# A Flamingo layer on one core: context columns by DMA and 32x32 blocks instead of TensorE, norms on ScalarE, head division in pairs

## The reference

```python
def reference(x, ctx, g_xattn, g_ffn, w_q, b_q, w_k, b_k, w_v, b_v, w_o, b_o, w_f, b_f):
    q, k, v = layernorm(x) @ w_q.T + b_q, ctx @ w_k.T + b_k, ctx @ w_v.T + b_v      # 16 heads of 32
    attn = softmax(where(causal, q @ k.T / sqrt(32), -inf))                         # per batch and head
    x = x + tanh(g_xattn) * ((attn @ v) @ w_o.T + b_o)
    y = fp6_blocks(layernorm(x))                   # scale = max|block of 32| / 7.5, nearest value of 6 bits
    return x + tanh(g_ffn) * (y @ fp6_blocks(w_f).T + b_f)
```

## Time and profile before

| | |
|---|---|
| profiled execution, its own time | 1426.4 us |
| its span, first to last instruction | 1424.4 us |
| TensorE (PE) busy | 1381.7 us, 97% |
| VectorE (DVE) busy | 1102.1 us, 77% |
| ScalarE (ACT) busy | 894.7 us, 63% |
| GpSimd (POOL) busy | 854.3 us, 60% |
| share of the 16 DMA engines, main queue | 41.6% |
| mean granted TensorE clock | 0.989 |

### The profile page before, as it was taken

One profiled execution on the slowest core, in us unless ns is written; L12 is line 12 of the kernel. 1 busy time (PEld: TensorE's weight loads), 2 busy tenths in 40 slices (PEclk: granted clock), 3 DMA queues, 4 the chain that ended last, 5 costly groups with the idle time before them and its releaser, 6 DMA issues.

```text
span 1424.4 us, 35124 instructions
## 1 busy us (share of the span) xinstructions
PE 1381.7 (97%) x10844; PEld 1220.1 (86%) x10844; DVE 1102.1 (77%) x4219; ACT 894.7 (63%) x2969; POOL 854.3 (60%) x1387
## 2 busy tenths in 40 slices
PE   6899999999999999999999999999999999999976
PEld 6788888888888888888888888888888888888865
DVE  5778787887788878778788778788778887877763
ACT  4566666666666666666666666666666666666651
POOL 2455665566665666666656566556666566666662
PEclk9999999999999999999999999999999999999988
DMA  8444434444434444434444443444443444443310
GB/s 255 107 112 106 117 93 120 115 128 107 119 90 118 118 125 118 108 94 116 118 119 124 108 114 97 116 117 128 107 119 93 115 117 125 118 111 90 86 51 29
DMA packets 156103, 159.10 MB, mean 112 GB/s; under 512 B 28176, under 2 KB 130576, under 8 KB 155920
## 3 DMA queue, kind: packets, MB, share of 16 engines
q1 hardware_dynamic: 155920, 156.87, 41.6%
HBM read 39.33 MB, written 16.78 MB: 39 GB/s over the span
## 4 chain that ended last, share of the span: by engine, by line
PE 91%; DVE 3%; SPq 2%; issue 1%; ACT 1%; POOL 1%; DMA 1%; DVEq 0%; ACTq 0%; POOLq 0%
PE proj L483 20%; PE proj L484 20%; PE proj L485 20%; PE pT_ps L533 12%; PE oT_ps L550 6%; PE proj L577 6%; PE s_ps L522 4%; PE s_ps L523 2%; SPq L342 1%; DMA all_probs<-in_L_xattn_w_v 1%; ACT all_probs L660 1%; DVE all_probs L807 0%; DMA q_stack<-q_hi 0%; POOL x L448 0%; POOL x L444 0%
## 5 line engine op out<-in xcount | busy, mean ns | idle before, releaser
L410 POOL TENSOR_TENSOR all_probs<-all_probs,rden 128x128 f32<-128x128 f32 (+1 forms) x1024 | 505.0, 514 | 473.3 <-DVE rden L867 472.1
L660 ACT ACTIVATE all_probs<-all_probs,neg_max 128x128 f32<-128x128 f32 (+1 forms) x1024 | 458.7, 451 | 396.7 <-DVE neg_max L807 396.5
L807 DVE CUSTOM_DVE_ANT_0 all_probs<-s_ps,causal 128x128 f32<-128x128 f32 (+1 forms) x1024 | 321.7, 351 | 164.4 <-PE s_ps L523 160.8
L533 PE MATMUL pT_ps<-ident,all_probs 128*128 128x128 f32 x1536 | 264.5, 282 | 6.6 <-POOL all_probs L410 4.3
L660 ACT ACTIVATION_READ_ACCUMULATOR all_probs<-all_probs,neg_max 128x1 f32 x1024 | 195.5, 191 | 0.0
L919 DVE COPY all_probs<-pT_ps 128x384 f32<-128x384 f32 x256 | 139.0, 543 | 66.5 <-PE pT_ps L533 66.5
L533 PEld LDWEIGHTS pT_ps<-ident,all_probs 128*128 128x128 f32 x1536 | 160.4, 142 | 21.7 <-issue 12.7
L522 PE MATMUL s_ps<-k_stack,q_stack 96*128 96x256 f32 x512 | 154.8, 302 | 2.8 <-DVE neg_max L807 2.2
L483 PE MATMUL proj<-cT_hi,wk_hi 128*128 128x256 f32 x512 | 153.2, 299 | 1.9 <-DVE cT_lo L861 1.1
L483 PE MATMUL proj<-aT_hi,wq_hi 128*128 128x256 f32 x512 | 148.0, 289 | 0.4 <-ACT vs L675 0.4
L484 PE MATMUL proj<-cT_lo,wk_hi 128*128 128x256 f32 x512 | 142.4, 278 | 0.0
(11 more groups left out here) (125 smaller groups left out, 3487.3 us busy)
## 6 DMA issues: line engine op xcount, KB each, us to landing
k_stack<-k_hi SPq DMA_DIRECT2D x512, 64.0 KB, 2.0
q_stack<-q_hi SPq DMA_DIRECT2D x512, 64.0 KB, 2.1
xs<-in_x SPq DMA_DIRECT2D x32, 512.0 KB, 4.2
cs<-in_ctx SPq DMA_DIRECT2D x32, 512.0 KB, 6.1
k_stack<-k_lo SPq DMA_DIRECT2D x256, 64.0 KB, 2.0
q_stack<-q_lo SPq DMA_DIRECT2D x256, 64.0 KB, 2.1
out<-x SPq DMA_DIRECT2D x32, 512.0 KB, 3.0
vs<-in_L_xattn_w_k SPq DMA_DIRECT2D x2, 512.0 KB, 7.0
```

Source lines behind the costliest of these rows:

```text
L410: last = nc.gpsimd.tensor_tensor(p, p, rden[:, sd, t, h:h + 1].to_broadcast([P, (1 + t) * P]), ALU.mult)
L533: last = nc.tensor.transpose(pT_ps[h % 2][:, m * P:(m + 1) * P], probs[:, h % P_RING, m * P:(m + 1) * P], ident[:, :])
L660: last = nc.scalar.activation(probs[:, h % P_RING, cols], probs[:, h % P_RING, cols], ACT.Exp, scale=-1.0, bias=neg_max[:, sd, t, h:h + 1] ...
L807: last = nc.vector.tensor_tensor_reduce(probs[:, h % P_RING, cols], s_ps[h % 2][:, cols], causal[:, (1 - t) * P:], 1.0, MASKED, ALU.add, A ...
```

## The change

- The context is no longer transposed on TensorE. Four DMAs bring it from HBM as `c_quads`: group g of 32 partitions holds columns 128g to 128g+127 of all tokens, in pieces of 512 bytes. VectorE's `transpose` (32x32 blocks, one instruction of 128x512 per half) makes `cols`; ScalarE writes `cT_hi` from it and GpSimd subtracts for `cT_lo` (before: VectorE, from PSUM).
- Both norms go from VectorE to ScalarE (`normalised`, Identity with a scale and a shift per token); GpSimd computes the shift with one more small instruction after each power.
- Reciprocals and divisions take two heads at once, in even slots; probabilities are transposed two heads at once, in even slots, 4 slots after the even head's score; the ring of probabilities has 6 places, not 4.
- q and k are stacked together: 24 DMAs of twice the size per batch instead of 48.
- x is loaded a second time for the residual, and `add_o` is added in place in `x1` (`xb`); `blk_up` is computed directly, with one instruction fewer per half. xT and dT have tiles of their own.
- New order of units over the slots, banks given out in turn, new slots for each stage (`AT`), weights spread over steps 0 to 2, loads of k, q and v weights from ScalarE's queue.

(Comments that name the engine are put in for the reader.)

```diff
-UNITS = [("cT", 0, 1), ("cT", 1, 1), ("q", 1, 2), ("dT", 0, 4), ("k", 0, 1), ("dT", 1, 4), ("f", 0, 4), ("xT", 0, 1),
-         ("f", 1, 4), ("xT", 1, 1), ("o", 0, 3), ("o", 1, 3), ("q", 0, 1), ("v", 0, 1), ("k", 1, 1), ("v", 1, 1)]
-SLOT_PARTS = (2, 4, 4, 1, 1, 5, 4, 2, 3, 4, 4, 1, 3, 3, 3, 2)
+UNITS = [("k", 1, 2), ("dT", 0, 4), ("q", 1, 2), ("f", 0, 4), ("xT", 0, 1), ("o", 0, 3), ("xT", 1, 1), ("k", 0, 1),
+         ("dT", 1, 4), ("q", 0, 1), ("o", 1, 3), ("f", 1, 4), ("v", 0, 1), ("v", 1, 1)]
+SLOT_PARTS = (2, 4, 2, 1, 2, 4, 2, 4, 2, 4, 3, 1, 2, 4, 3, 4)
+AV_SLOTS = (11, 3)
+AT = {      # stage: (steps after its batch's first, slot) of each half
+    "cT": ((1, 1), (1, 3)), "cT_hi": ((1, 3), (1, 5)), "cT_lo": ((1, 3), (1, 5)),
+    "moments": ((0, 11), (0, 13)), "rstd": ((0, 12), (0, 14)), "xn": ((0, 13), (0, 15)),
+    "xb": ((3, 3), (3, 7)), "rstd2": ((3, 8), (3, 14)), "y": ((3, 8), (3, 14)), "amax": ((3, 9), (3, 15)),
+    "scales": ((3, 11), (4, 0)), "scaled": ((3, 12), (4, 1)), "grid": ((3, 13), (4, 2)),
+    "xd": ((3, 15), (4, 4)), "xf": ((3, 9), (3, 15)),
+}
...
+            def stack_pair(b, half):            # SyncE
+                sp.wait_ge(left["k"], 2 * b + half + 1)
+                sp.wait_ge(left["q"], 2 * b + half + 1)
...
+                for j in range(GROUP):
...
+                    for r, (q_at, k_at) in enumerate(((0, 2), (1, 2), (0, 3))):
+                        sp.dma_start(stack[r * DK:(r + 1) * DK, :, at:at + 2, :].bitcast(F32),
+                                     qk[its, q_at:k_at + 1:k_at - q_at].bitcast(F32)).then_inc(stacked[half][j], 16)
...
+            def deviation(n, t, mom, var, rstd, shift, va, rs):        # GpSimd
+                pool.wait_ge(va, n)
+                nc.gpsimd.tensor_tensor(rstd[:, t:t + 1], var[:, t:t + 1], minus_half[:, t:t + 1],
+                                        ALU.pow).then_inc(rs, 1)
+                pool.wait_ge(rs, 2 * n - 1)
+                nc.gpsimd.tensor_scalar(shift[:, t:t + 1], mom[:, t, 0:1], rstd[:, t:t + 1], -1.0, ALU.mult,
+                                        ALU.mult).then_inc(rs, 1)
...
+                for s in range(SLOTS):                                 # GpSimd's step
+                    for b, t in due("rstd2", i, s):
+                        deviation(2 * b + t + 1, t, mom2, var2, rstd2, shift2, va2, rs2)
+                    for b, t in due("rstd", i, s):
+                        deviation(2 * b + t + 1, t, mom1, var1, rstd1, shift1, va1, rs1)
+                    b, h = pair_summed(i, s)
+                    if s % 2 == 0 and live(b):
+                        divide(b, h)
...
+                for s in range(SLOTS):                                 # TensorE's step
+                    if live(i - 2):
+                        scores(i - 2, s)
+                    units(i, s, 0, SLOT_PARTS[s] // 2)
+                    b, h = pair_turned(i, s)
+                    if s % 2 == 0 and live(b):
+                        transpose_probs(b, h)
+                        transpose_probs(b, h + 1)
+                    units(i, s, SLOT_PARTS[s] // 2, SLOT_PARTS[s])
+                    for b, r in weighed(i, s):
+                        weigh_values(b, r)
...
+                for s in range(SLOTS):                                 # ScalarE's step
+                    for unit_ended in ended(i, s):
+                        unit(*unit_ended)
+                    for b, r in put_out(i, s):
+                        output_hi(b, r)
+                    for b, t in due("y", i, s):
+                        second_norm(b, t)
+                    for b, t in due("grid", i, s):
+                        to_grid(b, t)
+                    for b, t in due("cT_hi", i, s):
+                        upper("cT", b, t, cT_hi, (("k", 2 * b), ("v", 2 * b)))
+                    if live(i - 2):
+                        exponentials(i - 2, s)
+                    b, h = pair_turned(i, s)
+                    if s % 2 == 0 and live(b):
+                        act.wait_ge(pT_done, HEADS * b + h + 2)
...
+                        nc.scalar.activation(probsT[:, h % AV_HEADS + 1, :], pT_ps[1][:, 0:3 * P],
+                                             ACT.Copy).then_inc(pT_odd, 1)
...
+                for s in range(SLOTS):                                 # VectorE's step
+                    if live(i - 2):
+                        maxima(i - 2, s)
+                    b, h = pair_summed(i, s)
+                    if s % 2 == 0 and live(b):
+                        reciprocals(b, h)
+                    b, h = pair_turned(i, s)
+                    if s % 2 == 0 and live(b):
+                        dve.wait_ge(pT_done, HEADS * b + h + 1)
...
+                        nc.vector.tensor_copy(probsT[:, h % AV_HEADS, :], pT_ps[0][:, 0:3 * P]).then_inc(pT_even, 1)
+                    for unit_ended in ended(i, s):
+                        unit(*unit_ended)
+                    for b, t in due("amax", i, s):
+                        block_maxima(b, t)
```

More of the change, by code:

```diff
@@ L38 @@
 FP6_BLOCK = 32
+QUAD = 32
 MASKED = 1e37
@@ new lines, in ended, with chunks_at, chunks_before, columns @@
+                if at_slot == (slot - 1) % SLOTS and part == PARTS[kind] - 1 and live(i - lag):
+                    yield kind, half, i - lag, proj[place_of[kind, 2 * (i - lag) + half] % BANKS]
+        def chunks_at(i, s):
+            for chunk in WEIGHT_TURNS.get((i, s), ()):
+                yield TURNED.index(chunk), *chunk
+        def chunks_before(i, s):
+            return chunks_at(i, s - 1) if s else chunks_at(i - 1, SLOTS - 1)
+        def columns(kind, t):
+            return cols[:, COLS.index((kind, t)), :, :]
@@ new lines, in weight_bank, with whole, pair_turned, pair_summed @@
+        def weight_bank(u):
+            return proj[place_of["w", u] % BANKS][:, :].rearrange("p (c k) -> p c k", c=KC)
+        def whole(w, rows=KC):
+            return 1 + max(TURNED.index((w, m)) for m in range(rows))
+        def pair_turned(i, s):
+            return i - (2 if s >= PT_LAG else 3), (s - PT_LAG) % SLOTS
+        def pair_summed(i, s):
+            return i - (2 if s >= 2 else 3), (s - 2) % SLOTS
+        def weighed(i, s):
+            for r, slot in enumerate(AV_SLOTS):
+                if s == slot and live(i - 2 - r):
+                    yield i - 2 - r, r
@@ L305, in fused_kernel, with put_out @@
+        def put_out(i, s):
+            for r, slot in enumerate(OUT_SLOTS):
+                if s == slot and live(i - 2 - r):
+                    yield i - 2 - r, r
         block = es.enter_context(nc.Block())
@@ L475, in _ @@
+            for i in range(STEPS):
+                step(i)
         @block.tensor
@@ L604, in unit, with units, step @@
                     last.then_inc(done[kind], 1)
-            def units(i, s):
-                for (u, part), its_slot in zip(parts, slot_of):
+            def units(i, s, first, end):
+                for u, part in parts[slot_of.index(s) + first:slot_of.index(s) + end]:
                     kind, half, lag = UNITS[u]
-                    if its_slot == s and live(i - lag):
-                        unit(u, part, kind, half, i - lag, i)
-            def step(i, ph):
-                if at(i, 2):
-                    pe.wait_ge(wlo_ok, len(WEIGHTS) * KC)
-                    pe.wait_ge(add_ok, 1)
+                    if live(i - lag):
+                        unit(part, kind, half, i - lag)
+            def step(i):
                 for s in range(SLOTS):
@@ L828, in unit, with first_moments @@
-            def unit(u, kind, half, b, pl, sd):
-                bank = proj[BANKS[u]]
-                if kind in ("q", "k"):
-                    dve.wait_ge(hi_ok[kind], 2 * b + half + 1)
-                    hi, lo, bias = (q_hi, q_lo, bias_q) if kind == "q" else (k_hi, k_lo, bias_k)
+                nc.vector.tensor_scalar(var[:, t:t + 1], mom[:, t, 1:2], LN_EPS, None, ALU.add).then_inc(va, 1)
+            def first_moments(b, t):
+                dve.wait_ge(x_in, 16 * (b + 1))
+                moments(2 * b + t + 1, t, xs, stats1, mom1, var1, st1, mo1, va1)
```

814 lines of the change are left out of this document (405 added, 409 removed), and 4 rows, old and new, of the table WEIGHT_TURNS.

## The result

| | before | after |
|---|---|---|
| median of the runs | 1426.3 us | 1497.6 us |
| span of the profiled execution | 1424.4 us | 1494.9 us |
| a step in the middle | 42.28 us | 44.11 us |

The ratio is 1.0496 (95% interval 1.0478 to 1.0515). The direction was forecast, 1447 us was not, and 1497.6 lies outside 1379 to 1480.

What follows compares the result with a forecast made beforehand. TensorE was taken to bound the middle; a step of 41.0 us list plus 2.35 stall, taken as 43.3, gave +29 over 28 steps, beginning -9, end +1: span 1445.4, forecast 1447 us, range 1379 to 1480.

Steps and rivals of the forecast that it cites:

- A stall of 2.35 us in slots 8 to 11: Each step, TensorE's weighing waits for a chain through xT's bank, GpSimd's shift and ScalarE's norm: 2.35 us, bounds 1.8 to 2.8.
- TensorE's own list falls by 1.3 us to 41.0: Per step, fewer transposes and returns shorten TensorE's own work by about 1.3 us to 41.0 us, bounds 40.7 to 41.5.
- the 43.3 forecast: Middle step length in us, from 41.0 of TensorE's list plus 2.35 of stall; 1.03 us above the kernel before.
- The returns, five times 0.08 us less: Returns from transposes to matmuls on TensorE go from 17 to 12 a step, saving 0.4 us.
- The 0.3 us set against it for pairs of heads: Two heads' transposes in a row may leave gaps on TensorE: 0 to 0.6 us for 8 pairs, 0.3 taken.
- In the kernel before every cut shows: Argument for no stall: TensorE is at nine tenths throughout, so every cut in its work shortens the time.
- rival A: No stall, TensorE's list alone decides each step: 46 us less, 1381 us; chance 0.28.
- The beginning gives 9 us back: First steps: half of the idle in the first 71 us is won, -9 us, bounds -20 and +8.
- The end, +1: After the middle steps, one more full step at +1 us; the rest has slack.
- B: Slots 8 to 11: a longer TensorE list leaves a stall near 1.2 us that cancels the gain; 1417 us, chance 0.12.
- C: SyncE's stack issues are late for k_hi in slot 9: near 1485 us at 1.1 us an issue, 1535 at 1.25; chance 0.10.

Runs made afterwards that it cites:

- e1: The changed kernel with VectorE taking xT's lower half ahead of o's addition and moments in slot 8: 1515.7 us.
- e3: The changed kernel with VectorE taking xT's lower half before o's addition, and half 0's second norm in later slots (power 9, norm 10): 1457.1 us.
- e8: The kernel before with half of a slot's parts placed between the scores and the head's transposes: 1455.9 us, ratio 1.0199.
- e9: e7 with the pair of heads' transposes directly behind the scores of its slot instead of between the slot's parts: 1427.9 us.
- e7: e3 with a 32-byte spacer tile in front of add_o, putting its tiles at multiples of 64 bytes: 1448.9 us.
- e11: The kernel before with one of four transposes of each context half from batch 2 on (those outputs wrong): 1427.6 us, ratio 1.0001.
- e10: e9 with the first loads reordered, x first on SyncE, then the context, q's and v's weights later, ScalarE only k's: 1425.8 us.
- e12: e10 with o's weight transposes in slots 13 and 14 of step 1, f's singly in slots 12 to 15 of step 2: 1422.8 us.
- e16: The kernel before with VectorE's norm of x in slot 14 instead of 15, plus e11's edit (those outputs wrong): 1410.4 us, ratio 0.9882.
- e6: The kernel before with a 32-byte spacer tile in front of add_o, so its tiles lie off multiples of 64 bytes: 1438.6 us, ratio 1.0078.
- e4: e3 with no stacks issued on SyncE's queue from the third batch on (those outputs wrong): 1457.3 us.
- e14: e12 with VectorE adding for o first and taking o's moments last, and both heads' scores of a pair in the even slot: 1414.5 us.

## Why the prediction was off

- *A stall of 2.35 us in slots 8 to 11, one chain through xT's bank and ScalarE's norm.* Right in kind and in the chain's times: the weighing came 10.19 us after head 4's transposes, and e1 moved it as the chain demands. The stall is what the chain has over TensorE's list. As that list took 8.1 us in this stretch and not 7.85, 2.0 us were left.
- *TensorE's own list falls by 1.3 us to 41.0.* This is the step that failed: the list fell by 0.2, to 42.1 (e3). What the sum took off for transposes and returns did come, 1.7 us. Put at nothing, without a row that shows it, were the extra of 0.052 us where a part follows scores (15 a step, 0.8; the spacings of e3 show it, e8 the same in the kernel before, and e9 takes 8 of the 15 away) and the wider spacing of all parts (0.55, of which the 32 bytes account for 0.24, e3 to e7; the rest is open), and 0.2 where scores follow a weighing. A step thus came out 1.1 - 0.35 = 0.8 us above the 43.3 forecast, 28 of them 22 us.
- *The returns, five times 0.08 us less.* A misreading of the earlier trace rows. The first matmul behind transposes does take 0.08 us more, but the last transpose before it takes 0.03 us to its successor where the others take 0.11, so a return costs nothing. The 0.3 us set against it for pairs of heads nearly cancelled this in the sum.
- *In the kernel before every cut shows* (rival A). Wrong (e11), though without weight for the sum here: in e3 nothing waits in those slots, since the change also took x's norm and cT_lo from VectorE.
- *The beginning gives 9 us back.* It cost 16, another 25 us of the 50 missed. Up to the second weighing of slot 11 PE's recorded idle time is 35.5 us, and 20.9 in the kernel before, so idle time makes up 14.6 of the 16. Of the 35.5, VectorE ends 18.4, and 6.2 of the 20.9; loads end 10.0 and 9.6. The longest waits of the changed kernel up to 46 us are for loads, those from 46 to 126 us are of the weights' transposes, for banks and halves that VectorE has yet to deal with:

```profile
PE proj L532 <- DMA all_probs<-in_L_xattn_w_k: 5.0, 2, 4.6
PE oT_ps L537 <- DMA y<-in_L_xattn_b_v: 5.0, 1, 5.0
...
PE proj L511 <- DVE wv_lo L825: 2.1, 1, 2.1
...
```
```profile
PE proj L532 <- DVE qk L905: 3.8, 1, 3.8
PE proj L532 <- DVE wf_lo L825: 3.6, 1, 3.6
...
```

  I had counted idle slices as room, without a walk through the lists. By the medians x's place is worth 2 us (e10) and the weights' places 3 (e12); in e12's profile VectorE still ends 9.5 us of such waits. Which order of VectorE's list would remove the rest was not tried.
- *The end, +1.* +3.6: the last regular interval was 42.8 us, not 38.6. Beside the point.
- *Rivals.* A did not come: with the stall gone the list alone gave 42.1, not 41.0. B had the reason right, a longer list, but not its size: the stall was 2.0 us, not 1.2, and the gain it was to cancel was 0.2. C did not come; its sum had a slip too, since 1.1 us an issue gives 12 x 1.1 + 2 - 14.3 = 0.9 us a step, 1475 and not 1485.

## What to carry to other kernels

Price each boundary between kinds of matmul by a row in which exactly these two stand next to each other; a new order makes boundaries that the old trace does not have, and 0.052 us fifteen times in each of 28 steps is 22 us. Price both sides of a boundary, what comes before it and what comes behind. When the time of an experiment agrees with its forecast, count in the trace whether the reason does (e8). Before an edit that takes work off the busiest engine, look for the chain of the others that ends beside it: e11 shows a TensorE that is busy throughout with nothing to gain, in e16 the same transposes gave 12 us, once VectorE's norm stood a slot earlier. And compare the addresses of tiles when small ones are merged.

## What the runs showed of the hardware

- Shifting the tiles by 32 bytes off a multiple of 64 made the kernel before 0.78% slower (e6): 24 float32r matmuls of 256 columns took 2.80 us instead of 2.71. A DMA share of 0.16 instead of 0.48 changed neither the spacing nor the time (e4).
- Behind a head's scores the first matmul of a part takes 0.17 us to the next instead of 0.12 (e8, e14). A transpose behind scores takes 0.124 instead of 0.109.
- From the last float32 transpose to a float32r matmul behind it 0.03 us pass instead of 0.11, and this matmul takes 0.20 us to the next instead of 0.12 (256 columns), 0.32 instead of 0.23 (512): the change of kind costs nothing in sum (before, e3).
- VectorE's transpose of 128x512 in 32x32 blocks of float32 takes 1.14 us, ScalarE's Identity of 128x512 with a scale and a shift per partition 0.81.
- The granted clock falls to the lower level, 1.2 GHz, for some us in the first steps, at other places in one execution than in the next: from 26 to 30 us it is 1.00 in the changed kernel and 0.59 in e3, with the same instructions up to there.
